# Rows of running sums loaded as two 256 KB transfers a chunk instead of four of 128 KB, in a scan kernel with a mixture of experts

## The reference, cut to what matters

```python
x = silu(causal_conv(xn @ Wx.T))             # [B, L, 512]
b = (x @ Wb.T), c = (x @ Wc.T)               # 8 heads x 64 states
dt = softplus(x @ Wdt.T + b_dt)
state = exp(dt_t * a) * state + dt_t * b_t * x_t   # one step of the scan
y_t = c_t . state
out = (groupnorm(y + d * x) * silu(z)) @ Wout.T
g = silu(experts(xn));  result = input + out * g
```

## Time and profile before

| | us |
|---|---|
| median of three executions | 1201.6 |
| the profiled execution | 1209.2 |
| its span in the trace | 1207.4 |
| front, until the first rows of sums are issued | 189.6 |
| scan, until the own part of the last chunk | to about 760 |
| experts and output | to 1207.4 |

### The profile page before, as it was taken

How to read it: one execution, slowest core, us unless ns; L and a number is a source line. 1 busy time by engine, 2 the same in 40 slices (tenths; PEclk the granted TensorE clock), 3 DMA queues, 4 the chain that set the end, 5 groups by cost and what they waited for, 6 DMA issues and landing times.

```text
span 1207.4 us, 35027 instructions
## 1 busy us (share of the span) xinstructions
PE 1180.7 (98%) x13979; PEld 971.2 (80%) x13979; DVE 954.6 (79%) x2272; ACT 653.4 (54%) x1406; POOL 772.4 (64%) x727
## 2 busy tenths in 40 slices
PE   8999999999999999999999998999999999999998
PEld 4566668888888878888887887788888888899998
DVE  7999966899987778887887867887768776777776
ACT  6999985444445444444544445455455443555444
POOL 4889945545456567676667647467666655576774
PEclk9999999999999999999999998999999999999999
DMA  9698764543443434443443455465544446799894
GB/s 303 243 358 323 287 270 132 121 150 120 138 141 126 153 121 127 130 142 125 142 133 119 128 152 164 153 156 98 114 89 99 92 84 132 270 334 317 332 332 166
DMA packets 122450, 214.84 MB, mean 178 GB/s; under 512 B 22448, under 2 KB 80560, under 8 KB 117552
## 3 DMA queue, kind: packets, MB, share of 16 engines
q1 hardware_dynamic: 109136, 195.32, 47.7%
q0 software_dynamic: 12432, 17.11, 8.4%
q10 hardware_dynamic: 720, 0.18, 0.1%
HBM read 131.03 MB, written 81.53 MB: 176 GB/s over the span
## 4 chain that ended last, share of the span: by engine, by line
PE 85%; DVE 6%; ACT 3%; issue 2%; DMA 2%; SPq 1%; POOL 1%; ACTq 0%; POOLq 0%; DVEq 0%
PE ps L1414 27%; PE ps L1780 10%; PE ps L2290 8%; PE ps L2269 7%; PE ps L2054 6%; PE ps L1504 3%; PE ps L815 3%; PE ps L2056 3%; PE ps L1493 3%; PE ps L1481 3%; PE ps L1516 3%; PE ps L1436 2%; PE ps L683 2%; PE ps L631 2%; DMA x_dram<-x_early 1%
## 5 line engine op out<-in xcount | busy, mean ns | idle before, releaser
L1964 POOL DMA_INDIRECT ffn_dram<-ob,idx x64 | 108.4, 1694 | 83.4 <-DVE ob L1883 71.2
L1364 ACT ACTIVATE decay<-tap,ncum 128x64 f32<-128x64 f32 x344 | 87.0, 335 | 131.8 <-POOL tap L1265 131.8
L1270 POOL TENSOR_TENSOR x_lo<-x,x_hi 128x512 fp32r<-128x512 f32 x56 | 75.7, 1351 | 79.0 <-ACT x_hi L1343 79.0
L1293 POOL TENSOR_SCALAR yb<-x,dcol 128x512 f32<-128x512 f32 x64 | 45.5, 711 | 106.6 <-DMA y_dram<-yb 56.2
L2054 PE MATMUL ps<-dn,mid_hi 128*128 128x512 f32 x288 | 104.7, 398 | 0.6 <-DVE moments L1854 0.6
L2012 ACT ACTIVATE mid<-ps,b_up 128x512 f32<-128x512 f32 x96 | 65.9, 690 | 69.2 <-PE ps L1780 59.5
L1414 PE MATMUL ps<-x_hi,w_hi_b 128*128 128x512 f32 x240 | 98.8, 412 | 0.0
L1414 PE MATMUL ps<-x_hi,w_hi_c 128*128 128x512 f32 x240 | 98.4, 410 | 0.0
L2145 POOL TENSOR_SCALAR yc<-yc,gn_scale,gn_shift 128x512 f32<-128x512 f32 x56 | 75.8, 1366 | 32.0 <-DMA yc<-y_dram 32.0
L1414 PE MATMUL ps<-x_hi,w_lo_b 128*128 128x512 f32 x240 | 94.3, 393 | 0.0
L1414 PE MATMUL ps<-x_lo,w_hi_c 128*128 128x512 f32 x240 | 94.0, 391 | 0.0
(11 more groups left out here) (328 smaller groups left out, 3850.8 us busy)
## 6 DMA issues: line engine op xcount, KB each, us to landing
x_dram<-x_early SPq DMA_DIRECT2D x16, 1024.0 KB, 5.6
yc<-y_dram SPq DMA_DIRECT2D x16, 1024.0 KB, 6.8
y_dram<-yb SPq DMA_DIRECT2D x30, 512.0 KB, 3.2
x<-x_dram SPq DMA_DIRECT2D x26, 512.0 KB, 4.7
tap<-cum_half_dram SPq DMA_DIRECT2D x86, 128.0 KB
tap<-cum_dram SPq DMA_DIRECT2D x86, 128.0 KB
rows_dram<-xn SPq DMA_DIRECT2D x16, 512.0 KB, 3.3
ffn_dram<-zero SPq DMA_DIRECT2D x64, 128.0 KB
```

Source lines behind the costliest of these rows:

```text
L1270: nc.gpsimd.tensor_tensor(x_lo[b % 2][:, m, :], x2[b % NX][:, m, :], x_hi[b % 2][:, m, :].bitcast(F32), ALU.subtract).then_inc(x_lo_ready, 1)
L1364: n = nc.scalar.activation(decay[g % 2][:, h, :], key_row[g % NR][:, h, :], ACT.Exp, bias=t.ncum[:, g, h:h + 1])
L1964: pool.indirect_dma_start(out=t.ffn_dram, out_offset=bass.IndirectOffsetOnAxis(ap=t.idx[:, e, h * HC + c:h * HC + c + 1], axis=0), in_=ob[ ...
```

## The change

Each pair of 128 KB transfers becomes one of 256 KB that writes all 128 partitions. The source pattern gets an outermost dimension of two (the two halves of the chunk, or the two groups of heads), and inside it the 2 KB row is repeated 64 times with a step of zero. The destination is the whole tile. The bytes, the buffers, the places of issue and the readers stay. The readers now wait for two increments of 16.

```diff
         def load_cum(g):
             until(sp, exp_ready, g - NR + 1)
             until(sp, ecum_ready, g - NR + 1)
-            for j in range(2):
-                half = slice(j * HD, (j + 1) * HD)
-                sp.dma_start(key_row[g % NR][half, :, :], t.cum_half_dram[j, g].partition_broadcast(HD)).then_inc(
-                    cum_loaded[g % NR], 16)
-            for a in range(2):
-                half = slice(a * HD, (a + 1) * HD)
-                sp.dma_start(query_row[g % NR][half, :, :],
-                             t.cum_dram[g, a * MT:(a + 1) * MT, :].partition_broadcast(HD)).then_inc(
-                    cum_loaded[g % NR], 16)
+            keys = t.cum_half_dram[:, g].unsqueeze(1).to_broadcast([2, HD, H, HD])
+            sp.dma_start(key_row[g % NR], keys).then_inc(cum_loaded[g % NR], 16)
+            queries = t.cum_dram[g].rearrange("(a m) n -> a m n", a=2).unsqueeze(1).to_broadcast([2, HD, MT, P])
+            sp.dma_start(query_row[g % NR], queries).then_inc(cum_loaded[g % NR], 16)
@@ causal(g)
-            pool.wait_ge(cum_loaded[g % NR], 4 * loads(g, NR))
+            pool.wait_ge(cum_loaded[g % NR], 2 * loads(g, NR))
@@ exp_rows(g)
-            act.wait_ge(cum_loaded[g % NR], 4 * loads(g, NR))
+            act.wait_ge(cum_loaded[g % NR], 2 * loads(g, NR))
```

## The result

The changed kernel takes 1453.91 us (median of six executions, 1449.91 to 1457.67) against 1201.8 us of the kernel before beside it, a ratio of 1.2087 with a 95% interval of 1.2069 to 1.2105. It is 252 us slower. The forecast was 1467 us, with 1390 to 1620 us as the range.

The account below looks back on a forecast made before the run. TensorE was taken to set the scan's pace, 8.84 us a chunk; two DMA engines would need 12.8 us, 827 us of work in all, moving the last own parts from 760.07 to 1025 us: +265 us, so 1467 us, range 1390 to 1620 us.

Parts of the forecast that it names:

- The term that decides: Sums' loads in the scan: two DMA engines carry them, 12.8 us a chunk against TensorE's 8.84 us.
- The rate: Bytes one DMA engine moves during the scan: 23.5 GB/s taken, bounds 20.3 and 25.6 GB/s.
- the 6 us for gates and gathers: Small-packet transfers in the two engines' scan work, estimated at some 6 us of the 827 us.
- They always have work: Two engines' queue between chunks: next load issued 6.4 us after a landing, while another holds them over 11 us.
- The slack of 5 us: Landing of the sums before ScalarE's copy and the matmuls into its bank: some 5 us late costs nothing.
- the rival "at least four engines": Sums' loads on 16 or at least four engines, 7.2 us hidden behind TensorE's 8.84 us: 1201 us; chance 0.13.
- The clock: TensorE's clock falls in scan waits: 1.5 us lost a chunk, hidden; 1750 us if throughout; chance above bounds 0.06.
- Issues: Two fewer SyncE issues per chunk, some 1.2 us, covered by its wait for TensorE: worth 0.
- Shares: Expected scan signs: DMA share about 0.28, 92 GB/s, TensorE busy about 70%.

Follow-up runs that it names:

- Two edits that shorten this loop: Changed kernel with the sums' loads issued ahead of the wait for turned x, 1427.69 us; or with stores of y on ScalarE's queue, 1431.87 us.

## Why the prediction was right, and where it wasn't

**The term that decides** was right: two engines carry the sums. The windows show the share of two engines, and the old transfers with an outermost count of two, and nothing else changed, cost the same 21%. The rule of the Trainium skill ("DMA: Bandwidth & Descriptors", "Why a DMA increments its semaphore by 16 and not by 1") gives two engines here; by that rule, the traces agree: shares of 0.13 at an outermost count of 2 and of 0.25 at 4, and bursts above 0.9 at 16.

**The rate** was taken as 23.5 GB/s and is 24.4 GB/s when the two never run dry. My choice between 20.3 and 25.6 was 4% low. The two engines' work was put at 827 us; 64 periods at the floor are 64 x 12.28 = 786 us, so this term was 41 us too large. Some 30 us of that are the rate; the rest includes the 6 us for gates and gathers, which came from no row and which no run shows.

**"They always have work"** was wrong. The two engines run dry: the pace lost 12.73 - 12.28 = 0.45 us a chunk, 27 us over 61 periods, of which the windows show 19 us directly (the rest may lie where other engines hold the share up). The way there is the chain from a late landing through GpSimd and ScalarE to TensorE and the next issue. The prediction had counted 6.4 us plus "a microsecond or two" for the store of y, against 11 us. The trace of the changed kernel has GpSimd waiting for that store up to 11.2 us at a time (between 300 and 720 us: total, times, longest):

```profile
POOL yb L1288 <- DMA y_dram<-yb: 132.8, 15, 11.2
```

Two edits that shorten this loop, independent of each other, both bring the pace to 12.3 us. This error of 27 us and that of 41 us have opposite signs, and that is why the pace of 12.8 us came so close to 12.73. That closeness is luck; the range would have held either way. Together they move the last landing from 1019 to 1005 us; it came at 981.48 + 19.13 = 1000.6 us, and the last own parts at 1005 us in place of 1025.

**The slack of 5 us and the rival "at least four engines"** were wrong, and this is the step to learn from. The rival said 7.2 us of transfers behind 8.84 us of TensorE are hidden, 1201 us. Measured were 50 us over the form with 16 rows outermost. Slack was read once, for ScalarE's copy in one chunk, as some 5 us. It held neither for the sums (with the store out of the way some 33 us were still lost, and sooner issue of the sums took 27 of them off) nor for what stands behind them, a store for which GpSimd waits ahead of work that TensorE needs. GpSimd waited for that store in the kernel before already; there it cost nothing, since moving it away changed nothing. Comparing rates tells where the floor is. Where TensorE is slower than the transfers, what counts is how late each transfer behind the slow one lands, and who waits.

**The clock.** It does fall in the gaps: after 600 to 602 us with no TensorE work the granted clock is 0.50, the 1.2 GHz level, from 603 to 606 us.

```profile
600.00:602.00 2.00, 0.00 (x0) 0.02 (x1) 0.08 (x1) 1.11 (x2) 0.00 (x0) 1.00 0.13 52
603.00:606.00 3.00, 3.00 (x8) 2.32 (x8) 0.00 (x0) 0.00 (x0) 2.86 (x5) 0.50 0.57 145
```

TensorE's busy time grew by 75 us, 1.2 us a chunk; the prediction's 1.5 us a chunk for half speed was near, and that it would be hidden behind the transfers too. At the floor it is, since the pace there is that of two engines that never stop. At four engines TensorE's busy time is 19 us over that with 16 rows outermost. That the clock adds to those 50 us, or to the 27 us above the floor, is likely but wasn't separated.

**Issues.** Two issues fewer per chunk are worth 0, as said: with 16 engines the merged form equals the old one.

**Shares.** Forecast were a DMA share of 0.28 and 92 GB/s; between 300 and 720 us the windows have 0.28 and 95. TensorE was to be busy about 70% and is at 79%: the mean granted clock there is 0.91, and half-speed matmuls count as busy for longer. The prediction's own 10.3 us of TensorE in a period of 12.8 us would have given 80%.

## What to carry to other kernels

Write a repeated source so that its outermost dimension is a multiple of 16 (16 and 64 were fast here, 4 and 2 slow), even at the price of more transfers; here two transfers over 64 repeated rows each beat one over 2 x 64 by 21% of the kernel. Look in the windows for a DMA share that stands still at k/16 with low bandwidth. And before calling a slower transfer hidden, list everything queued behind it on the same engines and who waits for each, since a queue's lateness is handed on to transfers that the edit never touched.

## What the runs showed of the hardware that I had not expected

Issuing itself slows down when two engines are loaded. In the changed kernel SyncE needs 2.84 us for the query rows and 5.00 us for the x behind them (above), where single issues mostly took 0.3 to 0.6 us before. Others take up to 8.7 us, and the longest 12.5 us. With four rows outermost they mostly take 0.3 to 0.6 us. The issuing engine seems to be held until there is room behind the slow transfers; no run tested that by itself.

Issuing the sums' loads half a chunk sooner makes the kernel before 1% slower (1213.36 us), though ScalarE waits for the sums only 0.3 us in all. TensorE's busy time between 300 and 720 us falls from 412 to 404 us and the share of unexplained "issue" in the chain doubles from 2% to 4%. No run tells why; that stays open.
